# Layer 0 of a four-layer graph network: unit counts leave PSUM through ScalarE as bf16, larger register loads, dense blocks loaded from another queue

## The reference

```python
msgs = edge_val[:, None] * x[edge_col]          # edge_col = dst here, edge_row = src
agg = jax.ops.segment_sum(msgs, edge_row, num_segments=N_NODES)
x = _layernorm(x + agg @ W.T, axis=-1)
```

## Time and profile before

| | us |
|---|---|
| three executions | 4153.31, 4163.15, 4158.33 |
| median | 4158.33 |
| profiled execution, its own time | 4150.73 |
| its span in the trace | 4149.5 |

### The profile page before, as it was taken

One profiled execution on the slowest core, in us unless ns is written; L12 is line 12 of the kernel. 1 busy time (PEld: TensorE's weight loads), 2 busy tenths in 40 slices (PEclk: granted clock), 3 DMA queues, 4 the chain that ended last, 5 costly groups with the idle time before them and its releaser, 6 DMA issues.

```text
span 4149.5 us, 56706 instructions
## 1 busy us (share of the span) xinstructions
PE 3049.1 (73%) x17920; PEld 2113.4 (51%) x17920; DVE 2069.3 (50%) x7275; ACT 1087.8 (26%) x2612; POOL 2525.4 (61%) x2372
## 2 busy tenths in 40 slices
PE   3887777777767637779957996777667675798975
PEld 2665555455555525534434554565555543555543
DVE  7998788886666526432233224432322345222249
ACT  1344444454545525500040002400000035000016
POOL 3767666665555444267736771177777744777755
PEclk9999898998989868789967998888888887899985
DMA  6666666777666647478825673554444334877743
GB/s 242 80 120 92 126 129 127 141 144 144 141 140 136 155 87 222 148 193 240 235 82 155 196 200 84 165 158 135 138 135 136 114 104 168 274 217 220 215 123 107
DMA packets 485739, 639.73 MB, mean 154 GB/s; under 512 B 79146, under 2 KB 427524, under 8 KB 480708
## 3 DMA queue, kind: packets, MB, share of 16 engines
q0 software_dynamic: 153600, 258.41, 30.6%
q1 hardware_dynamic: 331844, 377.70, 28.9%
HBM read 427.79 MB, written 208.12 MB: 153 GB/s over the span
## 4 chain that ended last, share of the span: by engine, by line
PE 24%; POOL 24%; DVE 20%; issue 14%; DMA 10%; ACT 4%; DVEq 2%; SPq 1%; POOLq 0%; ACTq 0%
POOL rows_buf L723 23%; PE PSA L754 6%; DVE accT L1169 5%; PE PSA L528 4%; DMA T<-S 3%; PE PSA L772 3%; DMA accT<-Awd 3%; DVE rows_buf L1003 2%; PE PSA L1137 2%; DMA rows_buf<-T,idx 2%; PE PSA L1038 2%; DVE accT L1177 2%; PE PSA L1219 2%; DVE big L1123 2%; DVE stat L536 1%
## 5 line engine op out<-in xcount | busy, mean ns | idle before, releaser
L1292 POOL DMA_INDIRECT A<-rows_buf,big x572 | 896.2, 1567 | 532.1 <-ACT rows_buf L1064 252.7
L723 POOL DMA_INDIRECT rows_buf<-T,idx x888 | 841.3, 947 | 293.7 <-issue 273.3
L772 PE MATMUL PSA<-S,rows_buf 128*128 128x128 bf16 (+2 forms) x5904 | 593.0, 262 | 359.7 <-DMA rows_buf<-X,idx 204.0
L772 PEld LDWEIGHTS PSA<-S,rows_buf 128*128 128x128 bf16 (+2 forms) x5904 | 553.0, 151 | 436.4 <-issue 343.7
L823 DVE TENSOR_TENSOR accT<-PSA,accT 128x256 f32 (+2 forms) x354 | 132.8, 375 | 1212.9 <-PE PSA L772 1204.2
L723 POOL DMA_INDIRECT rows_buf<-X,idx x528 | 502.4, 952 | 312.0 <-issue 309.5
L1169 DVE TENSOR_TENSOR accT<-PSA,accT 128x784 f32 (+1 forms) x444 | 360.1, 811 | 229.0 <-PE PSA L1137 160.1
L1137 PE MATMUL PSA<-big 128*128 128x272 bf16 (+2 forms) x796 | 229.4, 362 | 231.5 <-DVE accT L1169 230.3
L1054 PE MATMUL PSA<-XRS,rows_buf 128*128 128x256 f32 x1144 | 312.5, 397 | 2.1 <-ACT rows_buf L1064 2.1
L1137 PEld LDWEIGHTS PSA<-big 128*128 128x128 bf16 x796 | 76.5, 121 | 336.8 <-DVE accT L1169 320.1
L754 PE MATMUL PSA<-XRS,rows_buf 128*64 128x512 bf16 (+3 forms) x912 | 242.9, 380 | 0.0
(11 more groups left out here) (273 smaller groups left out, 5650.0 us busy)
## 6 DMA issues: line engine op xcount, KB each, us to landing
XRS<-Ad SPq DMA_DIRECT2D x144, 512.0 KB
Ad<-accT SPq DMA_DIRECT2D x28, 1568.0 KB, 6.7
rows_buf<-Ad SPq DMA_DIRECT2D x72, 512.0 KB
XRS<-in_xpad SPq DMA_DIRECT2D x192, 128.0 KB, 3.9
rows_buf<-A SPq DMA_DIRECT2D x48, 512.0 KB, 4.5
A<-accT SPq DMA_DIRECT2D x3, 6272.0 KB
Awd<-accT SPq DMA_DIRECT2D x6, 3136.0 KB, 9.9
X<-rows_buf SPq DMA_DIRECT2D x144, 128.0 KB, 1.9
```

The source lines that it names most:

```text
L723: s_hg[i % RING].on(pool.indirect_dma_start(Gv(i % RING, j), None, table, bass.IndirectOffsetOnAxis(idx[:, c:c + 1], 0)), 16)
L772: last = pe.matmul(PS[i % 2][0:F, W * h:W * h + W], Gv(i % RING, j)[:, o:o + F], hits[:, i % SRING, j, :], start=j + part == 0, stop=j == ...
L1292: pool.indirect_dma_start(A, bass.IndirectOffsetOnAxis(tgt[:, c:c + 1], 0), G[:, i % RING, j, :], None, compute_op=ALU.add).then_inc(s_k[n ...
```

## The change

Units with `copied` set (all 192 hot ones, and of the cold ones those with an odd number in the order, 126) are copied by ScalarE from AB into SBUF as bf16 (`unit_copy`). VectorE then adds that copy and not AB, and TensorE's next unit waits for the copy (s_ac) and not for the addition (s_ae). Hot copies have two buffers, cold ones one, in the second half of XRS. The weighted part is as before. The waits of `onehots` on TensorE are left out where VectorE has already added the unit in question (`built`). Register loads take 14, 13 and 16 values for 7, 7 and 8; in all there are 52 loads for 93 in the stage. The dense blocks from the third on are loaded from ScalarE's queue behind `dense_turned`, and no longer in `transfers`.

```diff
+for u in UNITS:
+    u.copied = u.hot or u.at % 2 == 1
...
-        def dense_load(t):
+        def dense_load(e, t):
             r = rows(t)
             if t >= 2:
-                s_tp.of(sp, ("dense", t - 2))
+                s_tp.of(e, ("dense", t - 2))
...
             if p == DENSE0 + 1:
                 load_dense_rows()
-            for t in range(NT):
-                if dense_step(t) + 1 == p:
-                    dense_load(t)
+                for t in range(2):
+                    dense_load(sp, t)
...
-            if i % 7 == 0:
+            if i % 14 == 0:
...
+        def built(q):
+
+            if q.at >= spread.evicted:
+                v.wait_ge(s_am, q.at + 1)
+                if q.hot:
+                    v.wait_ge(s_amw, q.hots + 1)
...
             if u.at:
-                pe.wait_ge(s_ae, u.at)
+                before = UNITS[u.at - 1]
+                if before.copied:
+                    pe.wait_ge(s_ac, before.copies + 1)
+                else:
+                    pe.wait_ge(s_ae, u.at)
...
+        def unit_copy(u):
+
+            if u.copied:
+                sc.wait_ge(s_am, u.at + 1)
+                before = last_copied(u)
+                if before is not None:
+                    sc.wait_ge(s_ae, before.at + 1)
+                to = ABS[:, u.copies % 2, 0:NT * u.n] if u.hot else ABW[:, 0:NT * u.n]
+                sc.activation(to, AB[:, 0:NT * u.n], ACT.Identity).then_inc(s_ac, 1)
...
-            v.wait_ge(s_am, u.at + 1)
+            if u.copied:
+                v.wait_ge(s_ac, u.copies + 1)
+                got = ABS[:, u.copies % 2, 0:NT * u.n] if u.hot else ABW[:, 0:NT * u.n]
+            else:
+                v.wait_ge(s_am, u.at + 1)
+                got = AB[:, 0:NT * u.n]
             aw = slots(Aw[buffer_of(u.w)])
-            v.tensor_tensor(aw, AB[:, 0:NT * u.n].rearrange("p (b s) -> p b s", s=u.n), aw, ALU.add).then_inc(s_ae, 1)
+            v.tensor_tensor(aw, got.rearrange("p (b s) -> p b s", s=u.n), aw, ALU.add).then_inc(s_ae, 1)
+            spread.evicted = u.at + 1
...
             for u in us[1:2]:
                 build_unit(u)
+                unit_copy(u)
...
                     dense_turn(t)
                     dense_turned(t)
+                    if t + 2 < NT:
+                        dense_load(sc, t + 2)
```

More of the change, by code:

```diff
@@ L95 @@
     u.place = sum(q.k for q in UNITS[:i])
+for u in UNITS:
+    u.copied = u.hot or u.at % 2 == 1
+for u in UNITS:
+    u.copies = sum(q.copied for q in UNITS[:u.at])
 FIRST = {w: next(u for u in UNITS if u.w == w) for w in range(NWIN)}
@@ L98, with last_copied @@
 TURN = {w: i for i, w in enumerate(ORDER)}
+def last_copied(u):
+    far = 2 if u.hot else 1
+    done = [q for q in UNITS[:u.at] if q.copied]
+    return done[-1] if done and not (u.hot and done[-1].hot) else done[-far] if len(done) >= far else None
 def unit_at(p):
@@ L940, in load_dense_rows @@
                 s_al[0].on(sp.dma_start(xw[:, w, :], a["xpad"][bass.ds(los[w], 128), :]), 16)
-        def dense_load(t):
+        def dense_load(e, t):
             r = rows(t)
             if t >= 2:
-                s_tp.of(sp, ("dense", t - 2))
-            s_ld[t % 2].mark(("dense", t), sp.dma_start(Dn[t % 2][0:r, :, :],
+                s_tp.of(e, ("dense", t - 2))
+            s_ld[t % 2].mark(("dense", t), e.dma_start(Dn[t % 2][0:r, :, :],
                                                         Awd[0:XWIN, 0:r, W * t:W * t + W].rearrange("w p s -> p w s")), 16)
@@ L1073, in degree_add @@
         def degree_add(i):
-            if i % 7 == 0:
+            if i % 14 == 0:
                 lo = G0 + i
                 spread.cold_los = nc.values_load_multi_w_load_instructions(
-                    base0[0:1, lo:min(lo + 7, NG)], engines=[ET.DVE], min_val=0, max_val=LAST,
+                    base0[0:1, lo:min(lo + 14, NG)], engines=[ET.DVE], min_val=0, max_val=LAST,
                     skip_runtime_bounds_check_because="held under LAST")[1]
@@ L1083, in degree_add @@
                 v.wait_ge(s_ha, min(i, G0))
-            dw = degB[:, bass.ds(spread.cold_los[i % 7], W)]
+            dw = degB[:, bass.ds(spread.cold_los[i % 14], W)]
             v.tensor_tensor(dw, PS[1][:, 0:W], dw, ALU.add).then_inc(s_da, 1)
         def hot_degree_add(i):
-            if i % 7 == 0:
+            if i % 13 == 0:
                 spread.hot_los = nc.values_load_multi_w_load_instructions(
-                    base0[0:1, i:min(i + 7, G0)], engines=[ET.DVE], min_val=0, max_val=LAST,
+                    base0[0:1, i:min(i + 13, G0)], engines=[ET.DVE], min_val=0, max_val=LAST,
                     skip_runtime_bounds_check_because="held under LAST")[1]
@@ L1104, in onehots @@
                 if p % CG == 0:
-                    if n >= 3:
-                        v.wait_ge(s_am, unit_at(p - 2 * CG - 1).at + 1)
+                    if n >= 2:
+                        built(unit_at(p - CG - 1))
                     four = srcm[:, c:c + CG].unsqueeze(1).broadcast_to([128, W, CG])
@@ L1109, in onehots @@
                     if u.hot:
-                        before = unit_at(p - CG - 1) if n >= 2 else None
-                        if before is not None:
-                            v.wait_ge(s_amw, before.hots + before.hot)
                         v.wait_ge(s_oq, n + 1)
@@ L1117, in onehots @@
                 if p >= OHRING:
[L1118 to L1121, removed]
+                    built(unit_at(p - OHRING))
                 width = NT * u.n
```

14 lines of the change are left out of this document (10 added, 4 removed).

## The result

| | before | after |
|---|---|---|
| median, us | 4157.8 (4153.3 to 4163.2, 8 runs) | 4180.1 (4169.5 to 4183.7, 8 runs) |
| ratio | | 1.0049, 95% interval 1.0039 to 1.0060 |
| profiled execution / span, us | 4150.7 / 4149.5 | 4181.8 / 4180.6 |
| granted TensorE clock, mean | 0.869 | 0.872 |
| VectorE / ScalarE busy, us | 2069.3 / 1087.8 | 2008.5 / 1259.8 |

The changed kernel is slower by 0.5%, 22 us. VectorE has 61 us less to do, ScalarE 172 us more, and the end comes later.

What follows compares the result with a forecast made beforehand. The prediction took VectorE, TensorE close behind, to bound the first stretch, and a TensorE-VectorE-TensorE chain through AB, broken by late blocks, the second. Terms summed to +39 us, giving a 4198 us median; own range 4165 to 4240, wider range 4060 to 4265.

Steps and rivals of the forecast that it cites:

- dense blocks: Second stretch: earlier loads from ScalarE's queue remove most of TensorE's 90.9 us wait; -75 us, between -40 and -92.
- register loads: Spreading stage: 52 larger loads for 93, priced by value from the trace; -7 us, between -25 and +5.
- copies behind clearings (27 + 27 + 13): Copies queued behind ScalarE's clearings: +27 us second stretch, +27 first-stretch hot clearings, +13 first-stretch cold ones.
- copies elsewhere (14 + 5 + 21 + 14): Late copies: +14 us hot steps with three or four units, +5 with two, +21 second-stretch cold steps, +14 first-stretch.
- The rival of the late blocks: Shared transfer engines set landing, not order of issue, so -75 becomes -20; 4253 us, 10%.
- The place in ScalarE's queue: The copies' 196 us fit ScalarE's idle time, but unit 1's copy stands behind the 1.3 us weights and comes late.
- cold steps of the first stretch: Before step 92: +0.6 us for each of 24 steps, +14, and +1.3 for each of 10 with cold clearings, +13.
- Cheaper additions: VectorE's additions from bf16 SBUF copies take 350 and 570 ns, saving at most 98 us of VectorE time.
- Copies free: Rival: ScalarE runs far enough ahead that no copy is late; -110 us, 4048 us, 22%.
- only the clearings free: Rival: VectorE lags far behind at the clearings, so they cost nothing; -28 us, 4130 us, 13%.
- no change: Rival: the terms cancel; 4158 us, 10%.
- hot loop worst: Rival: +0.9 us in each of 40 hot steps and +50 us for hot clearings; 4242 us, 8%.

Runs made afterwards that it cites:

- dense_only: The kernel before with only the loads of dense blocks 2 to 48 moved to ScalarE's queue; 4072.6 us, 0.9805 of the kernel before.
- time_only: The changed kernel without copies, ScalarE writing as many zeros at each of the 318 copies' places, with no waits either way; 4058.3 us, 0.9770 of before.
- time_wait: The changed kernel without copies, ScalarE writing zeros instead after waiting for each unit's matmuls, nobody waiting for it; 4058.3 us, 0.9777 of before.
- copy_first: The changed kernel with a step's second unit built and copied ahead of the next step's weights on ScalarE; 4090.6 us, 0.9852 of before.
- no_copies: The changed kernel with no unit copied, every addition reading PSUM, the other edits kept; 4055.0 us, 0.9763 of the kernel before.
- late_release: The changed kernel with TensorE waiting for the addition of the unit before, not for its copy; 4236.8 us, 1.0199 of the kernel before.
- waits_only: The changed kernel without copies and with register loads back at 7 and 8 values; 4059.6 us, 0.9777 of the kernel before.

## Why the prediction was right, and where its terms were off

The forecast was 4198 us, slower; measured were 4180 us, 18 us lower, inside its own range. The mechanism was right: late blocks go, and copies queued in ScalarE's order cost more than both gains. That the sum is so close is in part luck. The clearings were priced 22 us too high and the other copies 20 us too low, and the dense blocks gave back less waiting than was taken and a clock that was left at nothing. The line "copies elsewhere" is what is left of the 119 us, so the column adds up by construction.

| term | predicted, us | measured, us |
|---|---|---|
| dense blocks | -75 | -81 |
| register loads | -7 | -6, inside the intervals |
| fewer waits in the builders | not priced | -12 |
| copies behind clearings (27 + 27 + 13) | +67 | +45 |
| copies elsewhere (14 + 5 + 21 + 14) | +54 | +74 |
| sum | +39 | +20 |

**Dense blocks.** Right in mechanism, and in size partly by luck. The step that kept part of the 90.9 us back (in the earlier trace rows only 3.0 of 6.75 us return) was sound: in the traces 30 us of it came back as waits for additions, which leaves 61 of the 75 that were taken. Most of the rest of the 93 us by which the stretch is shorter in the traces goes with the clock, 0.97 for 0.89, which the prediction did not price. The rival of the late blocks is refuted by dense_only.

**The place in ScalarE's queue.** The prediction said that ScalarE's time fits and its place doesn't. time_only, time_wait and copy_first show this. It took unit 1's copy behind the weights for the cause, and undoing that one position is worth 82 us. Its price was too small: it weighed a lateness of 1.4 us against 0.8 us saved and a part given back for the next units, net 0.35 us for a hot step. What it left out for the hot steps is TensorE: the next unit product waits for the same copy, as the step above shows (0.49 us at 824.87), and with it everything else of the step; such waits sum to 122.1 us. That this makes up the difference in price is argued from the waits; no run parts TensorE's share from VectorE's. 82 and the 45 us of the clearings are together more than 119, so they overlap; no run has both edits, and how much of either is left without the other stays open.

**Hot and cold.** Hot copies cost 60 us where 46 were taken, cold ones 55 where 75 were. For the cold steps of the first stretch, 27 us were predicted and 12 measured.

**Cheaper additions.** Another mis-sized step. The estimate of 350 and 570 ns was the middle between "same fixed part" and "none", and was taken for all units. It holds for half of them. Where a unit's slot begins in its window follows from the data; worked out from `dst` for all 444 units and set beside the durations in the trace:

| units | slot offset even | slot offset odd | same units, no_copies (even / odd) |
|---|---|---|---|
| hot, copied (8 wide) | 365 ns (343 to 416), 86 | 607 ns (585 to 655), 106 | 559 / 620 ns |
| cold, copied (16 wide) | 568 ns (548 to 622), 57 | 725 ns (700 to 770), 69 | 974 / 977 ns |
| cold, from PSUM | 972 ns, 67 | 970 ns, 59 | 975 / 977 ns |

(Medians, in brackets least and most, then the number of units.) The ranges of the copied ones don't touch. For 106 of the 192 hot units the copy, which costs a hop, made the addition cheaper by 13 ns. The two additions of the step above are one of each: 0.61 and 0.35 us. The copied additions take 179.1 us of VectorE in all, and the same ones 237 us in the kernel without copies (the sum of their durations): 58 us less and not the 98 that stood as the most. That is shown by durations in the traces; in copy_first and late_release the same split stands, and over nine in ten of the 318 additions are within 30 ns of the changed kernel's. No run shifts the slots, so that an even offset everywhere would save 25 us of VectorE in the hot units (106 x 0.24) is an estimate.

**Register loads.** The sum came out, its price did not: 14 values on the spreading stage's line 1087 take 1581 ns in the median and not the 3172 of line 806, and a few loads of 7 us and more stay.

**The trimmed waits.** The sum had no term for them. They go with 12 us less, of which the traces show 4 in front of VectorE's instructions.

**Rivals.** "Copies free" falls with the 119 us of no_copies, "only the clearings free" with the 45 us behind them, "no change" with the interval, and "hot loop worst" (4242) with the time. What was forecast for the profile came: the waits for copies over 80 us (287.4), a first stretch 40 to 100 us longer (75), a second shorter by up to 60 (55), blocks awaited for under 10 us (0.5); the additions' 0.35 and 0.57 us came for even slots alone.

The fastest kernel measured that does the whole work is no_copies, with time_only, time_wait and waits_only inside its interval: 2.4% faster than the kernel before (0.9763), 2.8% than the changed one.

## What to carry to other kernels

An idle engine is a cheap place for work but not a cheap stop on the way between two others: price a hop by what stands ahead of it in that engine's queue, and ask what that in turn waits for. Here 318 operations beside the chain cost 3 to 6 us, inside the interval, and the same number inside it 119 us, of which 82 went when the copy moved ahead of four operations. A change of three parts whose sum is a small loss can hold a large gain, so run the parts apart. A transfer that stands behind another's wait should be moved to a queue that is clear. And read the clock of a stretch together with its waits: here the idle time in front of the dense blocks went with a lower clock behind it.

## What the runs showed of the hardware

- An addition of bf16 operands in SBUF on VectorE depends on where its rows begin: with the window's slots at an even bf16 offset 365 ns for 49 rows of 8 and 568 ns for 49 rows of 16, at an odd one 607 and 725 ns. The form that reads PSUM shows it for rows of 8 (559 and 620 ns in no_copies) and not for rows of 16 (974 and 977). The Trainium skill has two statements. The page VectorE: DVE Perf Modes, section Mode 2×_1P, asks for a 4-byte-aligned start if two results a cycle are to come; the trace agrees that it matters. The page Vector Engine (DVE) Microarchitecture Reference, section 5.1 Performance modes, says that 4-byte alignment makes no difference with two sources; for the time of these rows, one source contiguous and the other source and the result in rows at a pitch of 128, it does. The odd additions of 16 stay well under the PSUM form, 725 ns against 977; what sets their price stays open.
- Waits that are already met are mostly hidden: 577 of them, shown at 21 ns each, 12 us in sum, went with 4.4 us of VectorE's idle time in front of the instructions behind them (6.8 to 2.4 us, dense_only and waits_only).
- TensorE's granted clock fell to its lower level in or at most 1 us behind each of its 15 waits for a block: 126 us of 551 before, 24 of 458 in dense_only, where these waits are gone.
- Register loads of the same size differ: on line 1087 loads of 14 values took 1.3 to 1.6 us five times and 3.4 to 7.2 us five times in no_copies. The rows of both lines in the changed kernel (least, median, most in ns) show the same spread. What decides was not tested.

  ```profile
  L1087 DVEq TENSOR_LOAD <-base x11: 347/1581/7190, 72.6 to 1470.0; - x11
  L1179 DVEq TENSOR_LOAD <-big x37: 343/1099/8421, 78.1 to 1436.5; - x37
  ```
